# Attention of a fused transformer layer: nine slots a pair instead of ten, the turning of the normalised tokens spread over the slots at a pair's seam

## What is computed

```python
h = _L0_tok_ref(...)                        # (16, 128, 1024), a state-space kernel per channel
h = jnp.concatenate([h, txt], axis=1)       # 16 sequences of 205 tokens, 1024 wide
h = h + _L0_attn_ref(_layernorm(h), Wqkv, Wo)
h = h + _L0_ffn_ref(_layernorm(h), ...)     # router, low-rank experts, base matrix

qkv = hidden_states @ Wqkv                  # attention: 32 heads of 32, one shared k and v
scores = jnp.einsum('bqhd,bkd->bhqk', q, k) * scale
scores = jnp.where(causal, scores + alibi, NEG_INF)
attn = jnp.einsum('bhqk,bkd->bqhd', jax.nn.softmax(scores), v)
return attn @ Wo
```

## Time and profile before

| | before |
|---|---|
| median of 3 runs | 1736.79 us (1732.65 to 1740.34) |
| the profiled execution | 1738.08 us, span 1736.3 us, granted clock 0.945 |
| TensorE busy | 1507.8 us (87%) |
| VectorE busy | 1134.3 us (65%) |
| ScalarE busy | 737.2 us (42%) |
| GpSimd busy | 536.6 us (31%) |

### The profile page before, as it was taken

How to read it: one execution, slowest core, us unless ns; L and a number is a source line. 1 busy time by engine, 2 the same in 40 slices (tenths; PEclk the granted TensorE clock), 3 DMA queues, 4 the chain that set the end, 5 groups by cost and what they waited for, 6 DMA issues and landing times. The chain is left out here.

```text
span 1736.3 us, 31628 instructions
## 1 busy us (share of the span) xinstructions
PE 1507.8 (87%) x9700; PEld 1335.7 (77%) x9700; DVE 1134.3 (65%) x4142; ACT 737.2 (42%) x2624; POOL 536.6 (31%) x314
## 2 busy tenths in 40 slices
PE   0355399989999999999999769999999999999999
PEld 0355288878878787887888558888988888888887
DVE  7999378879788878879787854443444434344343
ACT  3455157777767767767878631011000010100100
POOL 1788314443534343443445400110101111010110
PEclk9877689999999999989999679999999999999999
DMA  6144455454554445445455341212112121211201
GB/s 200 37 89 93 103 98 109 80 83 96 80 103 73 104 72 108 73 75 100 79 117 88 103 171 47 73 37 72 48 60 72 36 72 40 69 66 43 73 32 40
DMA packets 110527, 139.63 MB, mean 80 GB/s; under 512 B 13156, under 2 KB 96484, under 8 KB 110040
## 3 DMA queue, kind: packets, MB, share of 16 engines
q1 hardware_dynamic: 110408, 138.41, 34.8%
HBM read 62.82 MB, written 40.30 MB: 59 GB/s over the span
## 5 line engine op out<-in xcount | busy, mean ns | idle before, releaser
L700 ACT ACTIVATE P<-P,nmax 128x128 f32<-128x128 f32 (+1 forms) x1024 | 434.3, 426 | 95.1 <-DVE nmax L790 88.9
L764 POOL TENSOR_TENSOR P<-P,rden 128x512 f32<-128x512 f32 (+1 forms) x256 | 329.2, 1308 | 451.5 <-DVE rden L796 451.4
L790 DVE CUSTOM_DVE_ANT_0 P<-sc,mask 128x128 f32<-128x128 f32 (+1 forms) x1024 | 292.4, 323 | 101.1 <-PE sc L612 94.7
L1126 POOL TENSOR_TENSOR h<-h,base_b 128x1024 f32<-128x1024 f32 (+1 forms) x26 | 84.2, 3240 | 637.4 <-DVE xn L1153 637.4
L642 PE MATMUL pr<-xT_hi,wq_hi 128*128 128x410 f32 x576 | 243.0, 422 | 0.0
L802 DVE COPY PTR<-pt 128x282 f32<-128x282 f32 x512 | 222.2, 435 | 30.3 <-PE pt L622 17.1
L1039 PE MATMUL b<-w_hi,x2T_hi 128*128 128x390 f32 (+3 forms) x624 | 214.8, 344 | 14.3 <-DVE h L1199 13.2
L1039 PE MATMUL b<-w_lo,x2T_hi 128*128 128x390 f32 (+3 forms) x624 | 212.4, 340 | 0.0
L1039 PE MATMUL b<-w_hi,x2T_lo 128*128 128x390 f32 (+3 forms) x624 | 212.0, 340 | 0.0
L642 PE MATMUL pr<-xT_lo,wq_hi 128*128 128x410 f32 x576 | 204.0, 354 | 0.0
L642 PE MATMUL pr<-xT_hi,wq_lo 128*128 128x410 f32 x576 | 202.9, 352 | 0.0
(11 more groups left out here) (174 smaller groups left out, 3049.1 us busy)
## 6 DMA issues: line engine op xcount, KB each, us to landing
Qs<-q_hi SPq DMA_DIRECT2D x128, 205.0 KB, 4.5
Qs<-q_lo SPq DMA_DIRECT2D x64, 205.0 KB, 5.5
att_dram<-att SPq DMA_DIRECT2D x64, 205.0 KB, 2.4
at<-att_dram SPq DMA_DIRECT2D x25, 512.0 KB, 4.6
h<-h_dram SPq DMA_DIRECT2D x25, 512.0 KB, 3.4
out<-h SPq DMA_DIRECT2D x25, 512.0 KB, 2.6
h_dram<-Y SPq DMA_DIRECT2D x64, 128.0 KB, 3.0
ht<-h_dram SPq DMA_DIRECT2D x16, 512.0 KB, 5.8
```

The costliest lines, as they stand in the source:

```text
L700: last = nc.scalar.activation(P[rows, j % 2, i, cols], P[rows, j % 2, i, cols], ACT.Exp, scale=-1.0, bias=nmax[at], accum_out=den[at])
L764: lastp = nc.gpsimd.tensor_tensor(w, w, r, ALU.mult)
L790: lastv = v.tensor_tensor_reduce(P[0:n, j % 2, i, cols], sc[i % 2][0:n, cols], mask[0:n, m], 1.0, 3.0e38, ALU.add, ALU.min, nmax[0:n, j % ...
L1126: nc.gpsimd.tensor_tensor(h2[0:n, par, :], h2[0:n, par, :], base_b[0:n, :], ALU.add).then_inc(biased, 1)
```

## The change

`SLOTS` becomes 9 and `"ln"` leaves `MAIN`; q0, q1, q2, kv, q3 to q7 take slots 0 to 8, and score slots are 5 to 12, so that slots 5 to 8 and the next pair's 0 to 3 hold the units and only slot 4 has none. A pair's tokens are now turned in eight chunks by channel (128 channels of all 410 tokens each: four transpositions, `turn_ln`), at steps 0, 1, 3, 4 and 6 of the last slot (8) of the pair before and steps 0, 2 and 4 of the pair's own slot 0 (`LN_AT`), behind the projection's three products of that step. ScalarE's part (`hi_ln`) comes one step later, VectorE's (`lo_ln`) two steps later and as the first thing of its step. The projections alternate between banks 0 and 1 (slot 8: bank 2), and the chunks use what is free, six of them bank 1. Pair 0's eight chunks stand ahead of its slot 0. The semaphores are split by purpose. `load_h` and `load_wo` come before `stack_q` in slot 1 of SyncE's program; the statistics start at step 14 and the normalisation at step 38.

```diff
-SLOTS = 10
+SLOTS = 9
...
-    MAIN = ["ln", ("q", 0), ("q", 1), "kv", ("q", 2), ("q", 3), ("q", 4), ("q", 5), ("q", 6), ("q", 7)]
...
+    MAIN = [("q", 0), ("q", 1), ("q", 2), "kv", ("q", 3), ("q", 4), ("q", 5), ("q", 6), ("q", 7)]
...
+    MAIN_BANK = [0, 1, 0, 1, 0, 1, 0, 1, 2]
+    VT_BANK = 2
     V_SLOT = 6
-    LN_HI_AFTER, LN_LO_AFTER = 1, 2
-    SCORE_SLOT = [5, 6, 7, 8, 9, 11, 12, 13]
...
+    LN_SLOT = SLOTS - 1
+    LN_AT, LN_BANK, FIRST_BANK = [0, 1, 3, 4, 6, 8, 10, 12], [0, 1, 0, 1, 1, 1, 1, 1], [i % BANKS for i in range(KC)]
...
+    SCORE_SLOT = [5, 6, 7, 8, 9, 10, 11, 12]
...
+            def turn_ln(p, i):
+
+                banks = banks_of(p)
+                if i == 0:
+                    pe.wait_ge(xn_ready, 4 * p + 4)
+                if banks[i] in banks[:i]:
+                    pe.wait_ge(ln_read, KC * p + max(k for k in range(i) if banks[k] == banks[i]) + 1)
+                else:
+                    wait_count(pe, main_read, SLOTS * p - 2 + banks[i])
+                for s, (c, t0, n) in enumerate(TILES):
+                    at = c * S + t0
+                    last = nc.tensor.transpose(pr[banks[i]][:, at:at + n], ht[0:n, s, i * 128:(i + 1) * 128], ident[0:n, 0:n])
+                last.then_inc(ln_turned, 1)
...
+                        chunk, pair = ln_chunk(slot, i, 0), ln_pair(p, slot, first, last)
+                        if chunk is not None and pair is not None:
+                            turn_ln(pair, chunk)
...
+            for i in range(KC):
+                turn_ln(0, i)
             visit(body)(pe)
...
+            def lo_ln(p, i):
+                dve.wait_ge(ln_hi, KC * p + i + 1)
+                v.tensor_tensor(xT[1][:, i, :], pr[banks_of(p)[i]][:, 0:PT], xT[0][:, i, :].bitcast(F32), ALU.subtract).then_inc(ln_read, 1)
...
+                        chunk, pair = ln_chunk(slot, i, 2), ln_pair(p, slot, first, last)
+                        if chunk is not None and pair is not None:
+                            lo_ln(pair, chunk)
                         if sj is not None:
                             bias_head(*sj, i)
```

More of the change, by code:

```diff
@@ L41 @@
 PT = 2 * S
-SLOTS = 10
+SLOTS = 9
 BANKS = 3
-BANK_USES = 18
 GH = 8
@@ L471, in attention_block, with ln_chunk, ln_pair, banks_of @@
     STACKS = 3
-    MAIN = ["ln", ("q", 0), ("q", 1), "kv", ("q", 2), ("q", 3), ("q", 4), ("q", 5), ("q", 6), ("q", 7)]
-    USE = {0: 8, 1: 9, 2: 11, 3: 12, 4: 14, 5: 15, 6: 16, 7: 17}
-    KV_USE, VT_USE = 10, 13
-    V_SLOT = 6
-    LN_HI_AFTER, LN_LO_AFTER = 1, 2
-    SCORE_SLOT = [5, 6, 7, 8, 9, 11, 12, 13]
-    def hi_count(use):
-        return use + 1 if use < VT_USE else use
+    MAIN = [("q", 0), ("q", 1), ("q", 2), "kv", ("q", 3), ("q", 4), ("q", 5), ("q", 6), ("q", 7)]
+    Q_SLOT = [MAIN.index(("q", k)) for k in range(KC)]
+    KV_SLOT = MAIN.index("kv")
+    MAIN_BANK = [0, 1, 0, 1, 0, 1, 0, 1, 2]
+    VT_BANK = 2
+    V_SLOT = 6
+    LN_SLOT = SLOTS - 1
+    LN_AT, LN_BANK, FIRST_BANK = [0, 1, 3, 4, 6, 8, 10, 12], [0, 1, 0, 1, 1, 1, 1, 1], [i % BANKS for i in range(KC)]
+    def ln_chunk(slot, i, after):
+        at = (slot - LN_SLOT) % SLOTS * GH + i - after
+        return LN_AT.index(at) if at in LN_AT else None
+    def ln_pair(p, slot, first, last):
+        if slot == LN_SLOT:
+            return p + 1 if last is False else None
+        return p if not first and last is not None else None
+    def banks_of(p):
+        return FIRST_BANK if isinstance(p, int) and p == 0 else LN_BANK
+    def last_in(banks, bank):
+        return max(i for i in range(KC) if banks[i] == bank)
+    SCORE_SLOT = [5, 6, 7, 8, 9, 10, 11, 12]
     def att_unit(slot, lag):
@@ L559, in body @@
                 for slot, main, sj, tj, aj in slots(p, first, last):
+                    if slot == 1 and last is False:
+                        sp.wait_ge(ln_turned, KC * p + KC)
+                        for s in range(4):
+                            load_h(p + 1, s)
+                    if slot == 1 and last is True:
+                        sp.wait_ge(ln_turned, KC * p + KC)
+                        for k in range(4):
+                            load_wo(k)
                     if last is None and slot == 1:
@@ L580, in body @@
                         stack_q(p - 1, 7)
[L581 to L584, removed]
                     if aj is not None:
@@ new lines, in turn_v @@
+            def turn_v(p):
+                wait_apart(pe, main_read, SLOTS * p, const_ready)
+                for c in range(2):
+                    nc.tensor.transpose(pr[VT_BANK][:, 64 * c:64 * c + HD], vT[96:128, c * S:c * S + CH], ident[96:128, 96:128])
+                    last = nc.tensor.transpose(pr[VT_BANK][0:TXT, 64 * c + HD:64 * c + 2 * HD],
+                                               vT[96:128, c * S + CH:(c + 1) * S], ident[96:128, 96:128])
+                last.then_inc(vt_turned, 1)
@@ L667, in main_step @@
[L667 to L671, removed]
+                        turn_v(p)
+                    if slot == 0:
+                        pe.wait_ge(ln_read, KC * p + last_in(banks_of(p), 0) + 1)
+                    elif slot == 1:
+                        pe.wait_ge(ln_read, KC * p + KC)
+                    elif slot == SLOTS - 1:
+                        pe.wait_ge(vt_read, p + 1)
+                    else:
+                        pe.wait_ge(main_read, SLOTS * p + slot - 1)
@@ L672, in main_step @@
+                if slot == 0 and i > last_in(banks_of(p), 0):
+                    pe.wait_ge(ln_read, KC * p + i + 1)
+                out = pr[MAIN_BANK[slot]][:, 0:PT]
                 if what == "kv":
-                    last = three(pr[use % BANKS][:, 0:PT], wkv, slice(0, 128), i)
+                    last = three(out, wkv, slice(0, 128), i)
                 else:
-                    last = three(pr[use % BANKS][:, 0:PT], wq, slice(128 * what[1], 128 * what[1] + 128), i)
+                    last = three(out, wq, slice(128 * what[1], 128 * what[1] + 128), i)
@@ L731, in body @@
                         if i == 0 and slot == 0 and not first:
[L732 to L737, removed]
+                            hi_part(p - 1, SLOTS - 1)
+                        if i == 0 and slot >= 1 and main is not None:
+                            hi_part(p, slot - 1)
+                        chunk, pair = ln_chunk(slot, i, 1), ln_pair(p, slot, first, last)
+                        if chunk is not None and pair is not None:
+                            hi_ln(pair, chunk)
                         if sj is not None:
@@ L749, in _ @@
             act.wait_ge(const_ready, 1)
+            for i in range(KC):
+                hi_ln(0, i)
             visit(body)(act)
@@ L909, in _ @@
                 ln_apply(0, s, link)
+            for i in range(KC):
+                lo_ln(0, i)
             visit(body)(dve)
```

100 lines of the change are left out of this document (33 added, 67 removed).

## The result

The changed kernel takes 1724.77 us (median of 6 runs, 1722.45 to 1726.18), the kernel before in the same comparison 1738.17. The ratio is 0.9927, 95% interval 0.9911 to 0.9944: 13.4 us faster, where 33.6 were forecast. The time lies inside the range (1691 to 1727), near its upper end, but the gain is 0.40 of the one forecast. The profiled executions show the same, spans of 1736.3 and 1724.4.

The account below looks back on a forecast made before the run. TensorE was taken to bound the attention, with time to win in its waits, half clock and small work. The terms for pairs, start and tail summed to -33.6 us, from 1738.1 to 1704; range 1691 to 1727.

Parts of the forecast that it names:

- pair 0: First pair: slots 9 and 0 fall away, a slot without units comes, slot 8 grows, slot 6 loses 2.2; -12.9 us.
- pairs 1 to 6: Pairs 1 to 5 go from 96.62 to 91.2 us each, -27.1, with 3 given back; pair 6 gives -5.7.
- pair 7: Last pair: slot 0 full in place of slot 9, slots 1 and 2 become full, slot 6 loses 2.1; +2.5 us.
- tail (the rest): After the pairs: one more unit is left; slot 0 grows by 3.4, slot 2 by 1.6; together +5.0 us.
- the 3 that I had given back: Pairs 1 to 5: 0.6 us a pair allowed for disturbances above the quiet pair's 94.3, since the jump stays.
- Slots 4 and 5 as before, 17.3: Slots 4 and 5 of a pair keep their time, 17.3 us together.
- I keep the jump's price of 3.1: Loop's jump, now in slot 0 between dense steps, still costs 3.1 us: 2.79 standstill on VectorE, the rest slower clock.
- SyncE's queue: Stacking in slots 1, 3, 6, 8 waits for the slot's last head, `store_att` behind it; both costed at nothing.
- The clock behind the jump: Slot 0 behind a jump: bounds allowed up to 2.7 us more, a whole slot at the lower clock.
- Slots 8 and 0: Full slots with five and three chunks at 0.35 each, plus waits: 11.7 and 10.8 us (13.9 with the jump).
- VectorE as the seam's bound: Rival, chance 0.12: split, masking and copy hold TensorE in slots 8 and 0; 1720 us if half, 1737 if all.
- the stacking wait: Rival, chance 0.06: a TensorE wait of 2.16 us a pair for stacking DMAs returns elsewhere; 1719, with clock dips 1733.

Follow-up runs that it names:

- The run with the old steps: The changed kernel with the statistics back at step 12 and the normalisation at step 36, loop kept: 1714.04 us, ratio 0.9861 to the kernel before.

## Why the prediction was wrong in size

The sum by its own steps, against the spans of the two profiled executions (33.6 forecast, 11.9 measured):

| step | forecast | measured |
|---|---|---|
| pair 0 | -12.9 | -15.0 |
| pairs 1 to 6 | -29.8 | -8.6 |
| pair 7 | +2.5 | +2.6 |
| start | +1.6 | +3.1 |
| tail (the rest) | +5.0 | +6.0 |

Pairs 1 to 6 carry the miss of 21.2: 10.7 in slots 4 and 5, 10.3 in the jumps, 5.4 in slots 0 and 8, 0.7 in slot 3, less 2.8 in the others, where slots 1 and 6 came out shorter, and less the 3 that I had given back for disturbances that did not come. That the time still lies in the range is luck: its upper end was made of waits of chunks and of the clock, and neither of the two large terms was among them.

- **"Slots 4 and 5 as before, 17.3"** failed by 1.8 a pair. I had named the move of the start by two steps and costed it for slots 2 and 3 alone. Two normalising instructions of 0.81 passed from slot 4, which masks nothing, to the first steps of slot 5, ahead of its first heads. That is slot 5's 1.3, by the order of the instructions. Slot 4 itself grew by 0.45: TensorE waits there for a copy that VectorE makes behind a late part of the reciprocal root, in the kernel after:

```profile
523.67 0.33 PE L640 MATMUL pt<-ident,P 128*128 128x128 f32 x1 [0.63 <-DVE PTR L837]
```

  The run with the old steps, which moves the start and the end together and does not part the two, has no such wait and gave both slots back their old length. Its gain happens to be the same 10.7 us: slot 3 gave 0.85 a pair besides, and slots 0 to 2 took some back.
- **"I keep the jump's price of 3.1"** failed by 2.1 a jump (5.2), and with it **SyncE's queue, "I cost both at nothing"**. I had seen that q6's stacking would wait for slot 8's last head, and asked only who waits for these DMAs. They run exactly while the instruction queue's two packets do, and these took 1.7 to 1.9 us in place of 0.6 to 1.0. Moved away, the standstill fell from 4.0 to 2.5 and the jump's price from 5.2 to 3.7, and without a jump the move was worth nothing. What makes up the 0.6 still above 3.1 is not shown; 3.1 was itself the price of a quiet jump, where the five of the kernel before cost 3.5 in the mean. Nor is it a standstill of all engines in the same way: TensorE runs on past the jump and stops for VectorE. I had held that the price stays. The Trainium skill's page "Runtime: NRT & Kernel Launch" (section "Instruction fetch mechanics") says that a taken branch whose target is not at hand forces a DMA fetch of it. The trace agrees, with two packets of the instruction queue in every standstill, and that the fetch is a DMA should have made me look at what other DMAs are in flight.
- The clock behind the jump was in the bounds. It is not fixed: 13.6 to 16.4 us for one and the same slot.
- Slot 2 (11.06 for 11.1), slot 6 without its wait (7.38), pair 7 and most of the tail came as worked out: reading from a slot which engine sets its pace, and adding the moved work to that engine, held. Slot 3 (10.61 for 10.5) came out near by luck: without the two steps of statistics it takes 9.76, not 10.01, and they cost 0.85, not 0.5. Slots 8 and 0 took 0.5 and 0.4 more than forecast: 0.06 a chunk on TensorE, 0.2 and 0.1 that go away with the loop's form, and in slot 0 the 0.4 of VectorE's chain, of which the forecast had 0.3 as a wait at chunk 6.
- Of the rivals, VectorE as the seam's bound is small (0.4 a seam), the stacking wait did not come back, and in the attention's pairs the clock fell only behind the jumps: in pair 3 no other slot is under 1.00. The Trainium skill's page "TensorE: Matmul & The Clock Gate" (Part 4: PE-mode transpose) says that transpositions do not count as activity in the way matmuls do. By that slot 8 could have gone down; with twenty of them more it kept 1.00, so here the rule does not decide.

## What to carry to other kernels

When an edit moves a DMA, ask not only who waits for it but what else is in flight where it lands; a loop's jump is such a place. When it moves the start of a side task by a few steps, follow the task's end too: the steps that cost are those that cross into a slot with more work. A loop on an engine-bound stretch can cost more than its standstill, since the clock may follow: here standstills of 2.3 to 2.8 and of 4.0 went with 3.5 and 5.2 us a jump. And compare a pair that no jump leads into before the whole gain of writing a loop out is put down to its jumps.

## What the runs showed of the hardware

- The standstill behind a jump depends on the DMA traffic: 2.3 to 2.8 us at a DMA share of 0.25 to 0.31, 4.0 to 4.1 at a share of 1.05 to 1.07, in each of five jumps of each kernel. Two packets of the instruction queue lie in each, of 0.6 to 1.05 us together in the first case and 1.7 to 1.9 in the second.
- TensorE does not stop at the jump itself: it began the next iteration's first scores at 470.94, 0.19 after the start of the last product of the iteration before, went through scores, a turned head and three products, and stopped only for VectorE.
- After a wait of TensorE of 2.15 to 2.39 us (q6's stacking behind the jump) the slot had a mean clock of 1.00, 0.88 or 0.89, or 0.79 in one and the same execution. After 3.9 us it was 0.90 in all five slots of the changed kernel, with 0.57 for the 4 us behind each restart, and 0.90 or 0.81 with the statistics at step 12, with 0.57 or 0.50. Of the two levels, 1.2 and 2.4 GHz, the lower one held for most or all of these 4 us.
